# Weighted copies of one edge set on GpSimd: three tensor-scalar operations or one tensor-tensor operation

## The chip, the core and the metric

The kernel runs on one core of a Trainium2 chip. The metric is the device time of one launch in microseconds (us). The core's engines run side by side, each through its own list of instructions, and meet at semaphores: TensorE (PE in the profile, its weight loads PEld) multiplies, VectorE (DVE) and ScalarE (ACT) work on tiles, GpSimd (POOL) does too, and SyncE (SP) issues most transfers.

## The reference, cut to what matters

Four graph layers run over one graph of 3125 nodes (256 features) and 50000 edges sorted by their target. Each layer sums source rows into target rows, plain or weighted by the edge:

```python
# layer 0, twice: agg = segment_sum(h[src], dst); agg / max(deg, 1) @ W_l + b + h @ W_r
# layer 1:
gathered = support[edge_col] * edge_val[:, None]
out = jax.ops.segment_sum(gathered, edge_row, num_segments=x.shape[0])
# layer 2: segment_sum of messages (node and edge features), then an MLP with two layer norms
# layer 3: segment_sum of the 32 largest features of each row, divided by the degree
```

With A[d, s] the number of edges from s to d, and B[d, s] the sum of their weights, every such sum over node rows is a product with A or B. The kernel builds both matrices first and then multiplies with them.

## The kernel before

The edges are cut into 391 tiles of 128. Targets are cut into 25 blocks of 128 nodes, each into 8 groups of 16, so there are 200 groups; each is built by one call of `build_pair` on PE, and the text calls it a pair (it is fed by two kinds of sets). A set of an edge tile is a 128x128 one-hot matrix S (which row an edge belongs to), three copies of S in which each edge's row is multiplied by one of three bf16 parts of its weight, and a one-hot matrix Q of columns. S times Q adds to the counts, each weighted S times Q adds to the weights. All of this lies in `ring`, a part of `e_buf`.

A pair has three parts in the order of PE:

- **first**: the last tile of the pair before, against the first 200 columns (4 matmuls of 200 columns);
- **rest**: the tiles of this pair alone, one in 181 pairs and two in 19, in a loop whose bounds are read from a table on the chip (4 matmuls of 400 columns for each tile);
- **middle**: the tile that this pair shares with the next position, held in `next_set(par, 0..3)` (4 matmuls of 400 columns).

Who makes what for pair n:

- VectorE (`hot_pair`): Q of the first part (L997, 200 columns), S of the middle set (L993, it releases GpSimd through `s_hotS`), then for each rest tile S (L993), S times the first weight part (L1013) and Q (L997, 400 columns), and last Q of the middle set (L997, 400 columns). It waits for `s_used`, so that a buffer is written again only two pairs later.
- GpSimd (`weigh_pair`, L620): the three weighted copies of the middle set. It first copies the tile's three weight columns into `w_col` (L623), drains, waits for S, and then multiplies S by each column (L628, three operations). PE waits for them at L1404. After the seventh pair of a block it also does a subtraction of 256 columns, `second` (L617), for the first layer.
- ScalarE: the other two weighted copies of a rest tile (L669, L670), and the copies of the finished groups out of PSUM (L659, L660).

Buffers alternate by `par`, and the order on every engine is the order of the code: no scheduler moves anything. Once in 8 pairs each engine reads the next 8 table entries. PE also does a transpose (L1412) and a small product (L1418, L1420) once a block. When the 200 pairs are done, PE goes on to the layers, in the same list of instructions.

Of the kernel before, what the change touches and what calls it, by code (L numbers as in the profile page):

```python
# [7 lines left out]
F32, F16, BF16, I32 = mybir.dt.float32, mybir.dt.float16, mybir.dt.bfloat16, mybir.dt.int32  # L8
# [3 lines left out]
P = 128  # L12
# [16 lines left out]
SETS = 4 * P  # L29
# [28 lines left out]
def build(nc, x, src, dst, edge_attr, edge_weight, w, out):  # L58
    ctx = ExitStack()
    with ctx:  # L60
        def sb(name, shape, dt):
            return ctx.enter_context(nc.sbuf_tensor(name, shape, dt))

        def sem(name):
            return ctx.enter_context(nc.semaphore(name))
# [41 lines left out]
        col = front[:, 0:6 * NCOL].rearrange("p (a t) -> p a t", a=6)  # L107
        C_T, C_S, C_Q, C_W0, C_W1, C_W2 = range(6)
# [4 lines left out]
        ring = e_buf[:, 0:RINGW].bitcast(BF16)  # L113
        assert RINGW <= e_partw + e_hotw
        late = {}
        at = NCOL
# [12 lines left out]
        iota1 = sb("iota1", [P, GW], F16)  # L129
        off_g = sb("off_g", [P, NG], F32)  # L130
        off_n = sb("off_n", [P, NT], F32)
        w_col = sb("w_col", [P, 2, 3], F32)
        e_raw = sb("e_raw", [P, EC, DE], F32)
        e_key = sb("e_key", [P, EC], F32)
        e_sum = sb("e_sum", [P, DE], F32)
# [56 lines left out]
        s_hotP = sem("weighted_s_of_pool_ready")  # L192
# [69 lines left out]
        def wait(e, s, v):  # L262
            if not isinstance(v, int):
                e.wait_ge(s, e.snap(v))
            elif v > 0:
                e.wait_ge(s, v)

        def long_loop(e, count):

            return nc.Fori(0, count, engines=[e.engine], hint_back_edge=True)  # L270
# [41 lines left out]
        def drained(e):  # L312

            def step(ins):
                e.drain()
            return step
# [17 lines left out]
        def span(ap, start, width):  # L334
            return ap[:, start:start + width] if isinstance(start, int) else ap[:, bass.ds(start, width)]
# [4 lines left out]
        def bounded(v, low, high):  # L340
            return nc.s_assert_within(v, low, high, skip_runtime_bounds_check_because="the table is clamped to it")
# [20 lines left out]
        def next_set(par, part):  # L362

            at = par * SETS + part * P
            return ring[:, at:at + P]

        def rest_set(i, part):

            at = REST_AT + i % SLOTS * SETS + part * P
            return ring[:, at:at + P]  # L370
# [14 lines left out]
        def pairs_of(e, kind, c, which):  # L385

            lo, many = (0, PER) if which == "rest" else (PER, PER) if which == "fixed" else (0, 2 * PER)
            at = c * (2 * PER) + lo  # L390
            _, packed = nc.values_load_multi_w_load_instructions(
                tab[0:1, at:at + many] if isinstance(c, int) else tab[0:1, bass.ds(at, many)],
                engines=[kind], min_val=0, max_val=ET * 512 + ET + 1,
                skip_runtime_bounds_check_because="the table is clamped to it")
            return packed
# [4 lines left out]
        def low_of(e, v):  # L400
            return bounded(e.snap(v & 511), 0, ET)
# [175 lines left out]
        @block.gpsimd  # L577
        def _(pool):
            chain = drained(pool)
            pool.memset(rows_i[:, 0, EB - 1, :], 0).then_inc(s_pad, 1)  # L580
            pool.memset(rows_i[:, 1, EB - 1, :], PAD_DST).then_inc(s_pad, 1)
            pool.memset(rows[:, 2, EB - 1, :], 0.0).then_inc(s_pad, 1)
            pool.memset(X[:, NT - 1, :], 0.0).then_inc(s_xpad, 1)
            pool.memset(e_raw[:, :, :], 0.0).then_inc(s_pad, 1)
            chain(pool.memset(ident[:, :], 0.0))
            pool.affine_select(out=ident[:, :], in_=ident[:, :], compare_op=ALU.not_equal, fill=1.0, base=0,
                               pattern=[[-1, P]], channel_multiplier=1).then_inc(s_const, 1)
            pool.iota(iota1[:, :], pattern=[[1, GW]], base=1, channel_multiplier=0,
                      allow_small_or_imprecise_dtypes=True).then_inc(s_const, 1)
            pool.iota(off_g[:, :], pattern=[[GW, NG]], base=0, channel_multiplier=0,  # L590
                      allow_small_or_imprecise_dtypes=True).then_inc(s_const, 1)
            pool.iota(off_n[:, :], pattern=[[P, NT]], base=0, channel_multiplier=0,
                      allow_small_or_imprecise_dtypes=True).then_inc(s_const, 1)
            pool.iota(nidx[:, :].rearrange("p (b k) -> p b k", k=2), pattern=[[2 * P, 2], [1, 2]], base=0,
                      channel_multiplier=2,
                      allow_small_or_imprecise_dtypes=True).then_inc(s_const, 1)
            pool.memset(zeros[:, :], 0.0).then_inc(s_const, 1)
            pool.memset(ea_now[:, :], 0.0)
            pool.memset(eps_outer, LN_EPS).then_inc(s_const, 1)
            pool.memset(eps_inner, LN_EPS_INTER).then_inc(s_const, 1)  # L600
            pool.memset(ones_row[:, :], 1.0).then_inc(s_const, 1)
            pool.memset(ring[:, REST_AT + (SLOTS - 1) * SETS:REST_AT + SLOTS * SETS], 0.0)
            pool.memset(col[:, :, 0:1], 0.0).then_inc(s_const, 1)

            pool.memset(ZH[0].rearrange("p (n k) -> p n k", k=ZW)[:, :, 2 * D:2 * D + 2], 1.0).then_inc(s_ones, 1)
            pool.wait_ge(s_rs, 1)
            chain(pool.tensor_scalar(h_all, rs_all, H_SCALE, None, ALU.mult))
            pool.tensor_tensor(shift_all, nmean_all, h_all, ALU.mult).then_inc(s_rs, 1)  # L610
            pool.wait_ge(s_prep, PREP_STEPS)
            pool.wait_ge(s_prep_pe, PE_TABLES + 2)

            def second(n):
                wait(pool, s_z0, n + 1 + CR)
                pool.sem_inc(s_made, 1)
                pool.tensor_tensor(span(ZH[0], n * ZW + D, D), own_row, span(ZH[0], n * ZW, D), ALU.subtract  # L617
                                   ).then_inc(s_z2, 1)

            def weigh_pair(c, i, v):  # L620
                n, par = c * PER + i, i % 2
                w = w_col[:, par, :]
                pool.tensor_copy(w, col[:, C_W0:C_W2 + 1, bass.ds(low_of(pool, v), 1)].rearrange("p a o -> p (a o)"))  # L623
                pool.drain()
                wait(pool, s_hotS, n + 1)
                pool.sem_inc(s_made, 1)
                for k in range(3):
                    m = pool.tensor_scalar(next_set(par, k + 1), next_set(par, 0), w[:, k:k + 1], 1.0,  # L628
                                           ALU.mult, ALU.mult)
                m.then_inc(s_hotP, 1)  # L630

            with long_loop(pool, NT) as c:
                packed = pairs_of(pool, mybir.EngineType.Pool, c, "fixed")
                for i in range(PER):
                    weigh_pair(c, i, packed[i])
                    if i == 6:
                        second(c)


            def mlp_sums(n):  # L640
                for l in range(3):
                    wait(pool, s_y, n * 3 + (l + 1))
                    pool.tensor_tensor(GT[l + 1], GT[l], YT, ALU.add).then_inc(s_g, 1)  # L643

            with pool.Fori(0, NT) as n:
                mlp_sums(n)
# [234 lines left out]
        def _(dve):  # L881
# [118 lines left out]
            def hot_pair(c, i, v, fixed_):  # L1000
                n, par = c * PER + i, i % 2
                k_reg = step_of[mybir.EngineType.DVE]
                wait(dve, s_used, n * 2 + 1)
                edge_cols(n, q_first(par), HW, high_of(dve, fixed_), s_hotQ)
                u = low_of(dve, fixed_)
                wait(dve, s_used, n * 2 + 2)
                edge_rows(next_set(par, 0), u, s_hotS)

                dve.reg_add(room, k_reg, 1)
                with dve.Fori(high_of(dve, v), end_of(dve, v)) as t:  # L1010
                    wait(dve, s_restused, dve.snap(room, min_val=1, max_val=1 << 20))
                    edge_rows(rest_set(i, 0), t, s_restS)
                    dve.tensor_scalar(rest_set(i, 1), iota1[:, 0:P], one(col[:, C_S, :], t), one(col[:, C_W0, :], t),  # L1013
                                      ALU.is_equal, ALU.mult)
                    edge_cols(n, q_rest(par), GW, t, s_restQ)
                    dve.reg_add(k_reg, k_reg, 1)
                    dve.reg_add(room, k_reg, 2)
                edge_cols(n, q_next(par), GW, u, s_hotQ)
# [683 lines left out]
```

## Time and profile before

| what | us |
|---|---|
| median of 3 runs (1706.76 to 1711.73) | 1709.41 |
| the profiled execution, its own time | 1709.9 |
| its span in the trace | 1708.1 |
| building the two matrices, from 47.7 to 480.0 in the trace | 432.3 |
| the same for one of the 25 blocks (8 pairs), mean | 17.3 |

Columns of the rows below: a group of instructions has its line, engine, operation, what it writes and reads, shapes and count, then busy us and mean ns of one, then the idle time of the engine before them and who ended it. A row of a timeline has its start, its length, and what ran, "x3" being three in a row put together; brackets tell of idle time before it and of who ended it. Starts and lengths are us from the start of the span. An operation's length begins when the engine takes it up, so it holds any time in which it stands and waits for its data; the next one is taken up some 0.08 us before the end of the one ahead.

### The profile page before, as it was taken

To read this page: it belongs to the slowest core of one execution; us is meant where nothing else is said; L and a number is where in the kernel's file an instruction comes from. 1 tells how busy PE (TensorE), PEld (TensorE's weight loads), DVE (VectorE), ACT (ScalarE), POOL (GpSimd) and SP (SyncE) were. 2 spreads that over 40 slices of the span, in tenths; PEclk is the share of its full clock that TensorE was granted. 3 is DMA by queue.
4 is the path that set the end of the run, shared out by engine and by line. 5 is a ranking of instruction groups with operands and counts; after the bars stand their busy time and mean duration, and the time that the engine had idled before them with its cause. 6 is when DMAs were issued, how large, how long until landed. Compare 5 with 4: busy or idle time off the path is not lost.

```text
span 1708.1 us, 41810 instructions
## 1 busy us (share of the span) xinstructions
PE 1587.9 (93%) x11011; PEld 1227.7 (72%) x11012; DVE 960.3 (56%) x2841; ACT 625.3 (37%) x1718; POOL 326.2 (19%) x926
## 2 busy tenths in 40 slices
PE   2899999999988999899999999999899999977996
PEld 1555565555666777588878888888778888855885
DVE  5788888888842222233336666666537777773111
ACT  6677787777721111111112222222234444430000
POOL 1565565655610000000000000000011111110000
PEclk8899999999999999999999999999999999988998
DMA  4266676757696666333355655566322212211444
GB/s 133 70 179 170 156 193 164 186 155 195 163 255 202 193 193 194 127 120 130 122 161 155 178 160 159 163 179 174 108 82 80 76 64 80 80 39 62 150 153 152
DMA packets 353541, 245.55 MB, mean 144 GB/s; under 512 B 195243, under 2 KB 337383, under 8 KB 353511
## 3 DMA queue, kind: packets, MB, share of 16 engines
q1 hardware_dynamic: 353510, 245.19, 50.1%
q8 instruction: 14, 0.23, 0.1%
q14 instruction: 17, 0.13, 0.0%
HBM read 138.17 MB, written 99.31 MB: 139 GB/s over the span
## 4 chain that ended last, share of the span: by engine, by line
issue 60%; PE 33%; DVE 3%; POOL 2%; DVEq 1%; SPq 0%; POOLq 0%; DMA 0%; ACT 0%
PE ps L1377 21%; PE ps L1466 8%; POOL work L643 2%; PE ps L1420 1%; PE ps L1418 1%; DVE e_buf L997 0%; DVE work L943 0%; PE ps L1412 0%; PE ps L1639 0%; SPq L419 0%; PE ps L1353 0%; DVE small L1253 0%; PE ps L1365 0%; DVE e_buf L1013 0%; PE ps L1370 0%
## 5 line engine op out<-in xcount | busy, mean ns | idle before, releaser
L1466 PE MATMUL ps<-arena 128*128 128x256 f16 (+1 forms) x5000 | 605.3, 274 | 18.3 <-DVE arena L1317 8.9
L1466 PEld LDWEIGHTS ps<-arena 128*128 128x128 f16 x5000 | 488.1, 98 | 115.5 <-issue 47.2
L1377 PE MATMUL ps<-e_buf 128*128 128x400 bf16 (+1 forms) x2476 | 374.8, 308 | 23.6 <-DVE e_buf L997 23.5
L1377 PEld LDWEIGHTS ps<-e_buf 128*128 128x128 bf16 x2476 | 217.6, 98 | 169.6 <-DVE e_buf L997 51.6
L1460 PE MATMUL ps<-arena 128*128 128x256 f32 x1250 | 279.6, 381 | 0.6 <-ACT arena L791 0.6
L1460 PEld LDWEIGHTS ps<-arena 128*128 128x128 f32 x1250 | 236.5, 191 | 32.3 <-ACT arena L791 0.9
L628 POOL TENSOR_SCALAR e_buf<-e_buf,w_col 128x128 bf16<-128x128 bf16 x600 | 220.9, 382 | 162.5 <-DVE e_buf L993 156.1
L643 POOL TENSOR_TENSOR work<-work 128x256 f32<-128x256 f32 x75 | 54.4, 726 | 1000.7 <-ACT work L836 1000.7
L997 DVE TENSOR_SCALAR e_buf<-iota,off_g,front 128x400 bf16<-128x400 f16 (+1 forms) x619 | 222.3, 405 | 35.0 <-PE ps L1377 30.6
L993 DVE TENSOR_SCALAR e_buf<-iota,front 128x128 bf16<-128x128 f16 x419 | 111.4, 273 | 40.5 <-PE ps L1377 26.8
L669 ACT ACTIVATE e_buf<-e_buf,front 128x128 bf16<-128x128 bf16 x219 | 88.3, 403 | 106.8 <-DVE e_buf L993 106.4
L1142 DVE TENSOR_SCALAR rdeg<-ps 128x1 f32 (+1 forms) x25 | 4.0, 159 | 172.1 <-PE ps L1466 162.3
L660 ACT ACTIVATE arena<-ps 128x400 f32<-128x400 f32 x200 | 99.5, 498 | 0.0
L659 ACT ACTIVATE work<-ps 128x400 f16<-128x400 f32 x200 | 98.1, 490 | 1.3 <-PE ps L1377 1.3
L747 ACT ACTIVATE work<-ps 128x256 f32<-128x256 f32 x75 | 28.8, 383 | 175.7 <-PE ps L1440 175.7
L670 ACT ACTIVATE e_buf<-e_buf,front 128x128 bf16<-128x128 bf16 x219 | 85.3, 390 | 0.0
L1617 PE MATMUL ps<-work,front 128*128 128x128 f32 x600 | 81.6, 280 | 3.3 <-POOL work L643 3.2
L742 ACT ACTIVATE small<-small 128x1 f32<-128x1 f32 x50 | 14.7, 294 | 186.1 <-DVE small L1030 186.1
L1617 PEld LDWEIGHTS ps<-work,front 128*128 128x128 f32 x600 | 74.9, 196 | 7.0 <-POOL work L643 4.7
L1333 DVE SCALAR_TENSOR_TENSOR work<-ps,rdeg,arena 128x256 f32<-128x256 f32 x25 | 12.1, 484 | 113.2 <-PE ps L1466 113.2
L1013 DVE TENSOR_SCALAR e_buf<-iota,front 128x128 bf16<-128x128 f16 x219 | 75.1, 343 | 0.0
L836 ACT ACTIVATE work<-ps,mlp_col 128x128 f32<-128x128 f32 x150 | 46.8, 364 | 58.0 <-PE ps L1617 58.0
(214 smaller groups left out, 1580.4 us busy)
## 6 DMA issues: line engine op xcount, KB each, us to landing
arena<-turned_blocks SPq DMA_DIRECT2D x75, 800.0 KB, 4.3
wgt_blocks<-arena SPq DMA_DIRECT2D x25, 1600.0 KB, 10.3
arena<-wgt_blocks SPq DMA_DIRECT2D x25, 1600.0 KB, 8.3
cnt_blocks<-work SPq DMA_DIRECT2D x25, 800.0 KB, 5.6
turned_blocks<-arena SPq DMA_DIRECT2D x25, 800.0 KB, 3.5
e_raw<-edge_features_padded SPq DMA_DIRECT2D x25, 576.0 KB, 7.8
edge_features_padded<-in_edge_attr SPq DMA_DIRECT2D x24, 512.0 KB, 9.9
out<-arena SPq DMA_DIRECT2D x24, 128.0 KB
```

The lines of the kernel that those rows point to most:

```text
L628: m = pool.tensor_scalar(next_set(par, k + 1), next_set(par, 0), w[:, k:k + 1], 1.0, ALU.mult, ALU.mult)
L643: pool.tensor_tensor(GT[l + 1], GT[l], YT, ALU.add).then_inc(s_g, 1)
L659: act.activation(stage_c[par][:, t, :], cnt_ps[t % 2][:, 0:GW], ACT.Copy)
L660: act.activation(stage_w[par][:, t, :], wgt_ps[t % 2][:, 0:GW], ACT.Copy).then_inc(s_taken, 1)
L669: act.activation(rest_set(i, 2), rest_set(i, 0), ACT.Copy, scale=one(col[:, C_W1, :], t))
L670: act.activation(rest_set(i, 3), rest_set(i, 0), ACT.Copy, scale=one(col[:, C_W2, :], t)).then_inc(s_restA, 1)
L993: return dve.tensor_scalar(into, iota1[:, 0:P], one(col[:, C_S, :], t), None, ALU.is_equal).then_inc(s_S, 1)
L997: dve.tensor_scalar(into, iota1[:, 0:wide], one(off_g, n), one(col[:, C_Q, :], t), ALU.add, ALU.is_equal).then_inc(s_Q, 1)
L1377: return pe.matmul(bank[:, 0:wide], rows_, cols, start=start, stop=True, skip_group_check=True)
L1460: m = pe.matmul(agg[par][:, 0:D], BLK32[par][:, b * P:(b + 1) * P], ZFULL[0][:, b * D:(b + 1) * D], start=(b == 0), stop=(b == NT - 1), sk ...
L1466: m = pe.matmul(agg[par][:, 0:wide], BLK16[par][:, b * P:(b + 1) * P], ZH[zin(i)][:, b * ZW + part * D:b * ZW + part * D + wide], start=(b ...
L1617: m = pe.matmul(mlp_ps[:, o * P:(o + 1) * P], W[:, k, o * P:(o + 1) * P], GT[l][:, k * P:(k + 1) * P], start=(k == 0), stop=(k == 1))
```

## The change

GpSimd's three operations for a pair become one. Its first operand is S read three times over (a step of zero between the three), its second the three weight columns straight from `col`, each repeated over 128 columns, and it writes 3 x 128 columns in one go. `w_col`, the copy into it and the drain are gone. Nothing on another engine is touched.

```diff
-        w_col = sb("w_col", [P, 2, 3], F32)
...
+        def next_sets(par, part, many):
+
+            at = par * SETS + part * P
+            return ring[:, at:at + many * P]
+
...
             def weigh_pair(c, i, v):
                 n, par = c * PER + i, i % 2
-                w = w_col[:, par, :]
-                pool.tensor_copy(w, col[:, C_W0:C_W2 + 1, bass.ds(low_of(pool, v), 1)].rearrange("p a o -> p (a o)"))
-                pool.drain()
+                factors = col[:, C_W0:C_W2 + 1, bass.ds(low_of(pool, v), 1)].broadcast_to([P, 3, P])
+                plain = next_set(par, 0).rearrange("p (o n) -> p o n", o=1).broadcast_to([P, 3, P])
                 wait(pool, s_hotS, n + 1)
                 pool.sem_inc(s_made, 1)
-                for k in range(3):
-                    m = pool.tensor_scalar(next_set(par, k + 1), next_set(par, 0), w[:, k:k + 1], 1.0,
-                                           ALU.mult, ALU.mult)
-                m.then_inc(s_hotP, 1)
+                pool.tensor_tensor(next_sets(par, 1, 3).rearrange("p (a n) -> p a n", n=P), plain, factors, ALU.mult
+                                   ).then_inc(s_hotP, 1)
```

GpSimd's list of instructions, before, around the subtraction after a block's seventh pair (`s_ready` is the semaphore of the finished S; REGISTER_ALU and ISA are work of its sequencer, here the address of the tile's weight columns):

```order
L628 TENSOR_SCALAR e_buf<-e_buf,w_col 128x128 [waits s_ready]
L628 TENSOR_SCALAR e_buf<-e_buf,w_col 128x128 x2
L264 REGISTER_ALU
L617 ISA [waits first_part_ready]
L617 REGISTER_ALU
L617 TENSOR_TENSOR arena<-arena 128x256
L623 REGISTER_ALU
L623 ISA
L623 COPY w_col<-front 128x3
```

The same place after the change:

```order
L263 REGISTER_ALU
L630 REGISTER_ALU [waits s_ready]
L630 ISA
L630 TENSOR_TENSOR e_buf<-e_buf,front 128x384
L263 REGISTER_ALU
L621 ISA [waits first_part_ready]
L621 REGISTER_ALU
L621 TENSOR_TENSOR arena<-arena 128x256
```

The work on the address moved from ahead of the wait for S to behind it, and one operation of 384 columns stands where three of 128 stood.

## Rows read from the trace of the kernel before

**Rows 1.** The page, its head and busy times of the engines.
```profile
span 1708.1 us, 41810 instructions
PE 1587.9 (93%) x11011; PEld 1227.7 (72%) x11012; DVE 960.3 (56%) x2841; ACT 625.3 (37%) x1718; POOL 326.2 (19%) x926
```

**Rows 2.** Windows: start:end, length, engines' busy us, PE clock, DMA; the build.
```profile
47.00:480.00 433.00, 412.71 (x2671) 247.24 (x2671) 359.00 (x1259) 333.76 (x935) 266.91 (x825) 0.99 0.65 167
```

**Rows 3.** The chain that ended last, between 200 and 275 us: start, us, what.
```profile
204.96 0.62 PE ps L1418 x2
...
222.66 0.62 PE ps L1418 x2
...
238.33 0.62 PE ps L1418 x2
238.95 1.06 PE ps L1420 x4
240.01 8.53 PE ps L1377 x60
248.54 0.22 PE ps L1412 x2
248.76 5.16 PE ps L1377 x36
253.92 0.62 PE ps L1418 x2
```

**Rows 4.** Who waited for whom from 60 to 440 us: us, times, longest.
```profile
PE ps L1377 <- DVE e_buf L997: 17.0, 17, 1.1
```

**Rows 5.** Who waited for GpSimd's L628 in the whole span: us, times.
```profile
  PEld ps L1377: 0.2, 1
```

**Rows 6.** Timeline of VectorE, then of GpSimd, through one pair.
```profile
212.57 0.31 DVE L997 TENSOR_SCALAR e_buf<-iota,off_g,front 128x200 bf16<-128x200 f16 x1
212.81 0.24 DVE L993 TENSOR_SCALAR e_buf<-iota,front 128x128 bf16<-128x128 f16 x1
...
213.18 0.31 DVE L1013 TENSOR_SCALAR e_buf<-iota,front 128x128 bf16<-128x128 f16 x1
213.41 0.38 DVE L997 TENSOR_SCALAR e_buf<-iota,off_g,front 128x400 bf16<-128x400 f16 x1
213.72 0.42 DVE L997 TENSOR_SCALAR e_buf<-iota,off_g,front 128x400 bf16<-128x400 f16 x1
214.06 0.38 DVE L997 TENSOR_SCALAR e_buf<-iota,off_g,front 128x200 bf16<-128x200 f16 x1
214.35 0.24 DVE L993 TENSOR_SCALAR e_buf<-iota,front 128x128 bf16<-128x128 f16 x1
...
213.25 1.12 POOL L628 TENSOR_SCALAR e_buf<-e_buf,w_col 128x128 bf16<-128x128 bf16 x3 [0.56 <-DVE e_buf L993]
```

**Rows 7.** GpSimd's groups by shape, whole span.
```profile
L628 POOL TENSOR_SCALAR e_buf<-e_buf,w_col 128x128 bf16<-128x128 bf16 x600 | 220.9, 382 | 162.5 <-DVE e_buf L993 156.1 <-issue 6.3
L643 POOL TENSOR_TENSOR work<-work 128x256 f32<-128x256 f32 x75 | 54.4, 726 | 1000.7 <-ACT work L836 1000.7
...
L617 POOL TENSOR_TENSOR arena<-arena 128x256 f32 x25 | 16.3, 651 | 0.0
...
L610 POOL TENSOR_TENSOR arena<-arena 128x25 f32<-128x25 f32 x1 | 0.2, 229 | 0.1
```

**Rows 8.** GpSimd's sequencer at L623: count, ns least/median/most, first and last start.
```profile
L623 POOLq ALU_OP  x200: 32/35/45, 47.1 to 476.1; - x100
L623 POOLq FUSED_REGOPS  x200: 46/46/52, 47.2 to 476.2; - x100
```

**Rows 9.** Timelines of GpSimd and VectorE around two of the 25 subtractions L617.
```profile
64.26 0.66 POOL L617 TENSOR_TENSOR arena<-arena 128x256 f32 x1
...
64.27 0.70 DVE L993 TENSOR_SCALAR e_buf<-iota,front 128x128 bf16<-128x128 f16 x1
...
305.89 0.67 POOL L617 TENSOR_TENSOR arena<-arena 128x256 f32 x1
...
305.96 0.67 DVE L997 TENSOR_SCALAR e_buf<-iota,off_g,front 128x200 bf16<-128x200 f16 x1
306.56 0.41 DVE L993 TENSOR_SCALAR e_buf<-iota,front 128x128 bf16<-128x128 f16 x2
```

**Rows 10.** Timeline of VectorE at a block's first pair.
```profile
309.23 0.33 DVE L997 TENSOR_SCALAR e_buf<-iota,off_g,front 128x200 bf16<-128x200 f16 x1 [1.34 <-PE ps L1377]
```

## The prediction

> **What bounds the kernel now.** I read the page first, then the build alone, then its chain, its waits, and one pair as a timeline. The page shows a span of 1708.1 us with PE busy for 93% [rows 1]; the change touches only the build of the two matrices, the 433 us in which GpSimd makes the weighted copies. There PE is busy for 412.71 us and VectorE for 359.00 [rows 2], so two engines are close to the bound and GpSimd is not. The chain says how close: in a block without a split pair (a pair with two rest tiles) it is PE and nothing else. The block from 238.33 to 253.92 is 0.62 + 1.06 + 8.53 + 0.22 + 5.16 = 15.59 us, with no hole [rows 3]. Sixty matmuls of L1377 are five pairs, so a pair costs PE 8.53 / 5 = 1.71 us; the other 1.90 us of the block are the small products. The block from 204.96 to 222.66 has one split pair and takes 17.70. Where PE does wait, it waits for VectorE's L997: 17.0 us in 17 waits [rows 4]. For GpSimd's three products PE's weight loads waited once, for 0.2 us [rows 5]. Making GpSimd faster therefore buys nothing by itself; what counts is what GpSimd does to VectorE, which has to deliver a pair every 1.71 us.
>
> VectorE's slack is small. In the pair shown, the middle S starts at 212.81 and that of the next pair at 214.35: 1.54 us, against PE's 1.71 [rows 6].
>
> **What goes, and what stands in its place.** The copy and the drain leave GpSimd's list, 200 times each. They lie off the path [rows 5], so they are worth nothing. The three L628 took 1.12 us together [rows 6]. The new operation isn't in the trace; the nearest rows are GpSimd's other two-operand operations: 229 ns for 25 columns (L610), 651 for 256 (L617), 726 for 256 with both operands f32 (L643) [rows 7]. Through L610 and L617 a column costs (651 - 229) / 231 = 1.83 ns, so 384 columns take 651 + 128 x 1.83 = 885 ns. With L643 it is (726 - 229) / 231 = 2.15 ns, and 726 + 275 = 1001. I take 0.89, since L617 mixes f32 with a 16-bit operand as the new operation does. The low end is 0.65: no shorter than L617, although it has more columns. Repeated reads (steps of zero) are in no row; I price them as ordinary ones.
>
> The Trainium skill (GPSIMD Engine Reference, section 3.1) has 4497 ns for a two-operand addition of 2048 columns, 2.2 ns per column, as the floor of its shared read port. As an estimate that makes 384 columns 0.84 us; L643's rate here, 2.15, agrees. By 0.84 the sum below would be +28 in place of +37.
>
> A second effect comes from the order: the address of the weight columns is now worked out behind the wait for S. These are two steps of GpSimd's sequencer, 35 and 46 ns [rows 8], so the operation starts 0.08 later than L628 did. L628 started 213.25 - 212.81 = 0.44 after S did; the new one starts at 0.52 and ends at 0.52 + 0.89 = 1.41. Before, the third product ended at 0.44 + 1.12 = 1.56. PE gets its weighted sets a little earlier, so no new wait at L1404, and no gain there either.
>
> **What the long operation holds up.** This is the term that decides. L617 is the one two-operand operation that GpSimd runs in the build, and the rows beside it show what VectorE does meanwhile. L617 ran from 305.89 to 306.56. VectorE's L997 of 200 columns began at 305.96 and lasted 0.67, where the same shape takes 0.33 when left alone [rows 9, 10]: it ended 0.07 after L617 did. The other case is the same: L993 began 0.01 after L617 and lasted 0.70 in place of 0.24 [rows 6, 9]. VectorE didn't slow down, it stood until GpSimd was done. With three short operations VectorE slips one of its own between two of GpSimd's: L1013 took 0.31 and the two L997 0.38 and 0.42 beside the three L628 [rows 6]. With one long operation there is no such gap.
>
> The Trainium skill (SBUF — State Buffer, section "Who interferes with whom") has the rule: a VectorE instruction in a two-port mode and a GpSimd instruction lock each other out for the whole instruction, without sharing. The 0.67 agrees. By it the sum is the one below; if the two merely shared the port, VectorE would stay under 1.71 us and the sum would be zero.
>
> Now which instruction is caught. An L997 of 200 columns needs the port 0.26 after its start (0.33 less the 0.07 by which the held one outlasted L617). Applied to the pair shown, the new operation runs from 213.33 to 214.22. L1013 began at 213.18 and needs the port at about 213.44; the L997 of the rest tile began at 213.41 and needs it at 213.67. The L993 of 64.27 would have needed it within its 0.24 and was held, so GpSimd takes the port at most 0.2 after its start, here by 213.53. So L1013 gets through and L997 is caught, until 214.22. It ends 0.12 later (0.07, and 0.05 for 200 more columns: 0.38 against 0.33), and the next is taken up 0.08 before that, 0.04 after GpSimd's end. From there the order is as now: L997 of the middle set to L997 of the next pair 214.06 - 213.72 = 0.34, less the 0.04 by which that L997 was stretched (0.42 for 0.38), so 0.30; then to the next S 212.81 - 212.57 = 0.24 [rows 6].
>
> **The sum.** From S to S VectorE needs 0.44 + 0.08 + 0.89 + 0.04 + 0.30 + 0.24 = 1.99 us, over PE's 1.71: VectorE sets the pace. Two things are added in a block. L617 still holds one instruction for 0.67 in place of 0.33, +0.34; now PE's work covers it, then nothing does. And at a block's first pair VectorE idles for 1.34 while its sequencer reads the table [rows 10]; the row names PE, but the table is read there. While the engine is held for 214.22 - 213.67 = 0.55 its sequencer works ahead, so I count 1.34 - 0.55 = 0.8. A block takes 8 x 1.99 + 0.34 + 0.8 = 17.06 us in place of 15.59, +1.47. PE's 1.90 us of small products are hidden then. I take the same +1.47 for the blocks with split pairs, whose extra wait between the two tiles stays. 25 x 1.47 = 37 us. All later stages stand behind the build in PE's list, so they move as a whole. The profiled execution's own time was 1709.9, 0.5 above the median of the runs: 1709.9 + 37 = 1747, and 1709.4 + 37 = **1746** for the median.
>
> At 1.00 us the cycle is 2.10, the block 8 x 2.10 + 0.34 + 0.7 = 17.8, and the sum +56: 1765. At 0.65 it is 1.75; the block 14.0 + 0.34 + 1.0 = 15.3 is under PE's 15.59, and nothing changes: 1709. The break-even lies near 0.69 us for the operation.
>
> **The rivals.** *More is caught.* If GpSimd takes the port before L1013 does (a start 0.1 earlier is enough), L1013 is held and the rest L997 comes after it: 0.31 (213.41 to 213.72) less what is already counted, about 0.24 more per pair, 8 x 0.24 x 25 = 48 us: 1794. The same happens if the repeated operands make the operation some 0.25 us longer. Against it: L1013 got through although L628 had begun 0.07 after it.
>
> *Nothing is caught that counts.* If the operation is under 0.69 us, or takes the port more than 0.34 after its start, so that the rest L997 passes too, only the last L997 is held, the cycle is 1.99 - 0.31 = 1.68, and PE stays the bound: 1709. Against it: both rows of L617.
>
> *Faster.* Now GpSimd takes the port three times per pair and a copy's worth besides; one short take would leave VectorE freer than now. What there is to gain is PE's waiting for L997, 17.0 us in 380 [rows 4], 19 in the whole build; most of it belongs to the split pairs, whose second tile waits for the first. Half of it would give 1700. It decides from an operation near 0.6 us, which would be shorter than L617 with half as many columns again.
>
> That the change doesn't take place is no rival: the order shows one operation of 384 columns per pair.
>
> **How the numbers follow.** Forecast (one instruction held per pair, 1715 to 1770): 0.62. More held: 0.12. Nothing changes: 0.16. Faster: 0.10. The measurement can tell about 0.3%, 5 us, from no change. So slower 0.74, same 0.16, faster 0.10. The range reaches from 1709, the low end of the operation's price, to 1785, which takes in its high end and a third of the way to the case with more held; about 0.1 is left out on each side.
>
> **What would show it.** Right: L997 of 400 columns has a mean well over the 0.38 to 0.42 seen now, near 0.7 (every second one held to about 1.0); PE's waits for L997 grow from 17 us to some 50; a plain block takes about 17 us in the chain; GpSimd's new operation is near 0.89; all stages after the build keep their lengths. Wrong: the operation under 0.7, or a mean of L997 near today's; L1013 held instead of L997 (the dearer rival); or a granted clock in the build clearly under today's 0.99 [rows 2], which would add to PE's own time and isn't in the sum.

## The result and the profile after

The changed kernel takes 1754.58 us (median of 4 runs, 1750.62 to 1756.53) where the kernel before took 1708.09 on the same chip: a ratio of 1.0268, with an interval of 1.024 to 1.0296. It is slower by 46 us; the prediction had 1746, between 1709 and 1785. The profiled run took 1755.56, its span grew from 1708.1 to 1753.7, by 45.6.

In the new file the lines are shifted: L993, L997, L1013, L1377, L1412, L1418 and L1420 are now one higher, the subtraction L617 is L621, the reading of the table on VectorE is L395, and the new operation is L630. First the head of the page and its line of busy times, then the build alone as one stretch (columns as in rows 2: PE, PEld, DVE, ACT, POOL, granted clock, DMA share, GB/s).

```profile
span 1753.7 us, 41010 instructions
...
PE 1604.8 (92%) x11011; PEld 1226.3 (70%) x11012; DVE 1038.7 (59%) x2841; ACT 635.0 (36%) x1718; POOL 252.5 (14%) x326
```

```profile
48.00:534.00 486.00, 433.27 (x2672) 248.57 (x2672) 437.64 (x1259) 343.86 (x937) 193.26 (x225) 0.99 0.58 152
```

Against [rows 1, 2]: the build is 53 us longer (485.4 in place of 432.3, from 48.1 to 533.5), and the granted clock in it is 0.99 in both, so the clock has no part. GpSimd's busy time in the build fell by 74 us, from 266.91 to 193.26. VectorE's rose by 79, from 359.00 to 437.64, with the same 1259 instructions. GpSimd does its work faster, and VectorE pays for it. Which instructions pay is seen in the groups by shape. GpSimd over the whole span, after:

```profile
L630 POOL TENSOR_TENSOR e_buf<-e_buf,front 128x384 bf16<-128x384 bf16 x200 | 175.2, 876 | 291.9 <-DVE e_buf L994 291.9
...
L621 POOL TENSOR_TENSOR arena<-arena 128x256 f32 x25 | 19.0, 761 | 0.0
```

VectorE from 60 to 480 us, first after, then the two groups of before that answer to it:

```profile
L998 DVE TENSOR_SCALAR e_buf<-iota,off_g,front 128x400 bf16<-128x400 f16 x364 | 212.9, 622 | 0.0
L1014 DVE TENSOR_SCALAR e_buf<-iota,front 128x128 bf16<-128x128 f16 x190 | 83.3, 438 | 0.0
L994 DVE TENSOR_SCALAR e_buf<-iota,front 128x128 bf16<-128x128 f16 x364 | 79.3, 246 | 33.7 <-PE ps L1378 29.3 <-issue 4.0
L998 DVE TENSOR_SCALAR e_buf<-iota,off_g,front 128x200 bf16<-128x200 f16 x174 | 56.2, 323 | 8.8 <-PE ps L1378 4.8 <-issue 2.4
```

```profile
L997 DVE TENSOR_SCALAR e_buf<-iota,off_g,front 128x400 bf16<-128x400 f16 x410 | 164.7, 437 | 0.0
L1013 DVE TENSOR_SCALAR e_buf<-iota,front 128x128 bf16<-128x128 f16 x213 | 73.2, 343 | 0.0
```

The 400-column operation went from a mean of 437 ns to 622, L1014 from 343 to 438; S and the 200-column operation, made while GpSimd is idle, stand at 246 and 323. The timeline shows the two ways in which this comes about, in two pairs that follow each other (VectorE, then GpSimd; start, length, what ran, x2 and x3 being so many instructions in one row):

```profile
264.81 0.30 DVE L1014 TENSOR_SCALAR e_buf<-iota,front 128x128 bf16<-128x128 f16 x1
265.04 1.05 DVE L998 TENSOR_SCALAR e_buf<-iota,off_g,front 128x400 bf16<-128x400 f16 x1
...
267.36 0.88 DVE L1014 TENSOR_SCALAR e_buf<-iota,front 128x128 bf16<-128x128 f16 x1
268.16 0.37 DVE L998 TENSOR_SCALAR e_buf<-iota,off_g,front 128x400 bf16<-128x400 f16 x1
```

```profile
265.06 0.91 POOL L630 TENSOR_TENSOR e_buf<-e_buf,front 128x384 bf16<-128x384 bf16 x1 [1.36 <-DVE e_buf L994]
267.36 0.83 POOL L630 TENSOR_TENSOR e_buf<-e_buf,front 128x384 bf16<-128x384 bf16 x1 [1.39 <-DVE e_buf L994]
```

In the first pair L1014 passes in 0.30 and the 400-column L998 of the rest tile starts at 265.04, 0.02 before GpSimd's operation, and stands until that is done: it ends at 266.09, 0.12 after GpSimd's 265.97. That is the forecast's case. In the second L1014 itself starts with GpSimd, lasts 0.88, and the whole rest tile comes after it: the dearer rival. Of the 181 pairs with one rest tile, L998 of the rest tile was held in 128 and L1014 in 48 (both in 2 of them). GpSimd seems to wait too: 77 of its 200 operations took 0.83 us, the other 123, nearly all begun beside an L1014 that was still at work, 0.88 and more; the mean of 0.876 holds this time.

The chain of waits in a plain block, to be held against [rows 3] (start, length, what the end hung on):

```profile
245.57 0.62 PE ps L1419 x2
246.19 1.06 PE ps L1421 x4
247.25 3.74 PE ps L1378 x28
250.99 1.54 PE ps L1378 x8
...
253.99 1.03 DVE e_buf L998
255.07 1.53 PE ps L1378 x8
...
260.55 1.04 DVEq L395
...
263.16 0.62 PE ps L1419 x2
```

From 245.57 to 263.16 it is 17.59 us, where it was 15.59. It is no longer PE alone: the chain crosses to VectorE, and the two long pieces there are a held L998 of 1.03 us and, before the next block, 1.04 us in which VectorE's sequencer (DVEq) reads the table while another L998 is held, from 260.56 to 261.58. GpSimd isn't on it: the profile puts the held time down to VectorE. PE's own waits, 60 to 480 us, first before, then after, and below them who waited for L630 over the whole span:

```profile
PE ps L1377 <- DVE e_buf L997: 18.0, 18, 1.1
```

```profile
PE ps L1378 <- DVE e_buf L998: 45.7, 122, 1.1
```

```profile
  PEld ps L1378: 0.2, 1
```

PE waits for VectorE 122 times and 45.7 us, where it was 18 times and 18.0 us. For the weighted sets it waited once, 0.2 us, as before [rows 5].

**Part of it is given back after the build.** The build ends 53.5 us later in the trace, the program 45.6. The first work of VectorE after the build is the reciprocal degree; it waits for the last block of counts to come back from memory. Before, then after:

```profile
494.20 0.16 DVE L1142 TENSOR_SCALAR rdeg<-ps 128x1 f32<-128x1 f32 x1 [9.75 <-DMA cnt_blocks<-work]
```

```profile
544.47 0.16 DVE L1143 TENSOR_SCALAR rdeg<-ps 128x1 f32<-128x1 f32 x1 [6.57 <-DMA cnt_blocks<-work]
```

It comes 14.2 us after the end of the build before, and 11.0 after it now. The last store of counts is issued by SP, before and after, behind transposed loads:

```profile
467.32 12.95 SPq L472 DMA_TRANSPOSE arena<-cnt_blocks  x2
...
486.56 0.43 SPq L463 DMA_DIRECT2D cnt_blocks<-work  x1
```

```profile
517.53 12.82 SPq L476 DMA_TRANSPOSE arena<-cnt_blocks  x2
...
536.28 0.43 SPq L467 DMA_DIRECT2D cnt_blocks<-work  x1
```

That was 6.6 us after the end of the build and is 2.8 now: the store stands on SP's queue behind two transposed loads of the blocks before (12.95 us before, 12.82 after). They ended 0.3 us after the end of the build before, and 3.2 ahead of it now: a longer block hides more of them. When the opening of the first layer is over the shift is down to 47.7; the later stages differ by some 2 us in either direction, which I can't put to one cause.

### The profile page after: what moved, and what is told of

Same layout as the page of the kernel before. It is cut to its first block, busy times and chain, and to the rows that moved or that the text cites. A ratio compares the mean times of both kernels' runs of the same rounds, so it can differ in the third digit from the quotient of the medians.

```text
span 1753.7 us, 41010 instructions
## 1 busy us (share of the span) xinstructions
PE 1604.8 (92%) x11011; PEld 1226.3 (70%) x11012; DVE 1038.7 (59%) x2841; ACT 635.0 (36%) x1718; POOL 252.5 (14%) x326
## 4 chain that ended last, share of the span: by engine, by line
issue 60%; PE 25%; DVE 8%; DVEq 3%; POOL 2%; SPq 0%; POOLq 0%; DMA 0%; ACT 0%
PE ps L1378 14%; PE ps L1467 8%; DVE e_buf L998 4%; POOL work L644 2%; PE ps L1421 1%; DVE e_buf L994 1%; PE ps L1419 1%; DVEq L395 1%; DVEq L998 1%; DVEq L994 1%; DVE e_buf L1014 1%; DVEq L1011 0%; DVEq L1010 0%; DVE work L944 0%; PE ps L1413 0%
## 5 line engine op out<-in xcount | busy, mean ns | idle before, releaser
L1378 PE MATMUL ps<-e_buf 128*128 128x400 bf16 (+1 forms) x2476 | 394.9, 308 | 56.6 <-DVE e_buf L998 56.1
L998 DVE TENSOR_SCALAR e_buf<-iota,off_g,front 128x400 bf16<-128x400 f16 (+1 forms) x619 | 296.1, 525 | 10.8 <-PE ps L1378 4.8
L630 POOL TENSOR_TENSOR e_buf<-e_buf,front 128x384 bf16<-128x384 bf16 x200 | 175.2, 876 | 291.9 <-DVE e_buf L994 291.9
L1014 DVE TENSOR_SCALAR e_buf<-iota,front 128x128 bf16<-128x128 f16 x219 | 96.7, 442 | 0.0
```

The lines of the kernel that those rows point to most:

```text
L630: pool.tensor_tensor(next_sets(par, 1, 3).rearrange("p (a n) -> p a n", n=P), plain, factors, ALU.mult).then_inc(s_hotP, 1)
L998: dve.tensor_scalar(into, iota1[:, 0:wide], one(off_g, n), one(col[:, C_Q, :], t), ALU.add, ALU.is_equal).then_inc(s_Q, 1)
L1378: return pe.matmul(bank[:, 0:wide], rows_, cols, start=start, stop=True, skip_group_check=True)
```

## The experiments

The theory: one GpSimd instruction, from its start to its end, keeps VectorE's operations waiting that read SBUF as these do, and 0.88 us of that in one piece is more than VectorE's slack. The rivals: it is the two-operand kind, or the repeated reads, or the later start, whatever the length; or GpSimd's result is late for PE.

**Three short operations of the same kind.** The new operation is cut into three of 128 columns; the kind, the operands, the address worked out late and the missing copy stay. Only the repeated read of S goes with the cut; the next two kernels have it.

```diff
-                plain = next_set(par, 0).rearrange("p (o n) -> p o n", o=1).broadcast_to([P, 3, P])
...
-                pool.tensor_tensor(next_sets(par, 1, 3).rearrange("p (a n) -> p a n", n=P), plain, factors, ALU.mult
-                                   ).then_inc(s_hotP, 1)
+                for k in range(3):
+                    m = pool.tensor_tensor(next_set(par, k + 1), next_set(par, 0), factors[:, k, :], ALU.mult)
+                m.then_inc(s_hotP, 1)
```

> The one operation of 384 columns is cut into three of 128, each still two-operand and straight from the weight columns; nothing else differs from the changed kernel. Theory (one long hold of VectorE): three holds of about 0.25 us with gaps between them, one VectorE instruction passes in each gap; the L998 of 400 columns fall from a mean of 0.62 us to under 0.50; total within 10 us of the kernel before, 1708 to 1718. Rival (what costs is that GpSimd reads two operands, or that the address is worked out behind the wait, however long one operation is): both are unchanged, so the total stays near 1755.

Measured: 1711.21, against 1708.59 for the kernel before beside it, a ratio of 1.0015 (1.0002 to 1.0027). GpSimd's and VectorE's groups from 60 to 480 us, and PE's wait in the same stretch:

```profile
L630 POOL TENSOR_TENSOR e_buf<-e_buf,front 128x128 bf16<-128x128 bf16 x579 | 221.9, 410 | 183.0 <-DVE e_buf L994 183.0
```

```profile
L998 DVE TENSOR_SCALAR e_buf<-iota,off_g,front 128x400 bf16<-128x400 f16 x404 | 176.4, 473 | 0.0
```

```profile
PE ps L1378 <- DVE e_buf L998: 19.7, 27, 1.1
```

An operation of 128 columns takes 0.41 us, and not the 0.25 that was expected. So a pair keeps GpSimd busy for 3 x 0.41 = 1.23 us in place of 0.88, and still the loss is all but gone: L998 is back at 473 ns, PE waits 19.7 us. Busy time, kind of operation and late address are out as causes of the 46 us; the length of a single instruction is left, and the repeated read, which the next two kernels keep.

**How the loss grows with the length.** Two kernels with an instruction of middle length. In the first the two-operand operation makes two copies instead of three, and PE uses the second twice; in the second, which is the kernel before, one one-operand operation makes all three copies from the first weight part.

```diff
-                factors = col[:, C_W0:C_W2 + 1, bass.ds(low_of(pool, v), 1)].broadcast_to([P, 3, P])
...
+                factors = col[:, C_W0:C_W1 + 1, bass.ds(low_of(pool, v), 1)].broadcast_to([P, 2, P])
...
-                pool.tensor_tensor(next_sets(par, 1, 3).rearrange("p (a n) -> p a n", n=P), plain, factors, ALU.mult
+                pool.tensor_tensor(next_sets(par, 1, 2).rearrange("p (a n) -> p a n", n=P), plain, factors, ALU.mult
...
-                product(weights, GW, next_set(par, 3), q_next(par)).then_inc(s_used, 1)
+                product(weights, GW, next_set(par, 2), q_next(par)).then_inc(s_used, 1)
```

> GpSimd makes two of the three weighted copies in one operation of 256 columns; the third is left out, and PE multiplies the second copy twice, so all its work stays. Theory: the operation takes about 0.65 us, just under the break-even of 0.69 that the prediction gave, so most of the 46 us are gone: 1708 to 1719. Rival (any single two-operand operation in place of the three short ones costs the same): near 1755. If the cost is simply proportional to columns: 1739.

```diff
-                for k in range(3):
-                    m = pool.tensor_scalar(next_set(par, k + 1), next_set(par, 0), w[:, k:k + 1], 1.0,
-                                           ALU.mult, ALU.mult)
-                m.then_inc(s_hotP, 1)
+                plain = next_set(par, 0).rearrange("p (o n) -> p o n", o=1).broadcast_to([P, 3, P])
+                pool.tensor_scalar(ring[:, par * SETS + P:par * SETS + 4 * P].rearrange("p (a n) -> p a n", n=P), plain,
+                                   w[:, 0:1], 1.0, ALU.mult, ALU.mult).then_inc(s_hotP, 1)
```

> The kernel before with its three one-operand multiplications put into one of 384 columns with repeated reads; all three copies get the first weight part, so the weights differ. Copy and drain stay. Theory: what counts is how long one operation holds VectorE. Between 25 and 128 columns a column of a one-operand operation cost 0.8 to 0.9 ns, so it takes 0.57 to 0.62 us and the total stays at the kernel before, 1706 to 1713. Rival (any one long operation costs as much as the changed kernel's): 1750 and more. If it takes over 0.8 us the theory wants 1725 or more.

Measured: 1714.32, 1.0037 (1.0023 to 1.0051), for the first; 1714.72, 1.0034 (1.002 to 1.0048), for the second, a little over the range that was expected of it. GpSimd's group, 60 to 480 us, in the first and in the second:

```profile
L630 POOL TENSOR_TENSOR e_buf<-e_buf,front 128x256 bf16<-128x256 bf16 x191 | 122.0, 639 | 283.2 <-DVE e_buf L994 283.2
```

```profile
L628 POOL TENSOR_SCALAR e_buf<-e_buf,w_col 128x384 bf16<-128x384 bf16 x194 | 119.6, 617 | 247.5 <-DVE e_buf L992 247.5
```

An instruction of 0.62 to 0.64 us costs some 6 us, one of 0.88 costs 46: two thirds of the columns, an eighth of the price. That is a threshold and not a rate, as it must be where VectorE has slack to lose first. Beyond it nearly all counts: 0.876 - 0.639 = 0.24 us more in 200 pairs is 47 us, and 40 came. At this length it also doesn't matter whether the operation has one operand or two, nor whether it follows a copy; and both kernels read S repeatedly, so that alone isn't the cause either. The forecast's break-even of 0.69 was a little high, since 6 us are lost already at 0.62.

**The copy kept.** The new operation, with its factors from the copied weight columns; the copy and the drain are back, and no address stands between S and the operation.

```diff
+        w_col = sb("w_col", [P, 2, 3], F32)
...
-                factors = col[:, C_W0:C_W2 + 1, bass.ds(low_of(pool, v), 1)].broadcast_to([P, 3, P])
+                w = w_col[:, par, :]
+                pool.tensor_copy(w, col[:, C_W0:C_W2 + 1, bass.ds(low_of(pool, v), 1)].rearrange("p a o -> p (a o)"))
+                pool.drain()
+                factors = w.rearrange("p (a o) -> p a o", o=1).broadcast_to([P, 3, P])
```

> The one operation of 384 columns, but its factors come from the copied columns again, with the copy and the drain, so that no address is worked out behind the wait for S. This undoes the order part of the change alone. Theory: the operation starts 0.10 to 0.12 us earlier after S, the hold stays as long (0.87), and VectorE's cycle shortens by that much where it is held at the rest tile's L998: 8 x 0.1 x 25 = 20 to 24 us back, 1731 to 1736. Rival (the earlier start lets GpSimd take the port ahead of L1014 in most pairs, the dearer catch of the prediction): 1755 to 1790. Rival (copy and drain cost something of their own): slower than the changed kernel.

Measured: 1762.59, 1.0313 (1.0296 to 1.033). The theory's gain from an earlier start didn't come; the first rival did, and the second isn't ruled out. GpSimd's and VectorE's groups from 60 to 480 us (four lines were added ahead, so S is L998 here, L1018 the rest tile's S times the first weight part, and L1002 the 400-column operation), and one pair:

```profile
L634 POOL TENSOR_TENSOR e_buf<-e_buf,w_col 128x384 bf16<-128x384 bf16 x171 | 141.7, 829 | 223.8 <-DVE e_buf L998 223.8
```

```profile
L1018 DVE TENSOR_SCALAR e_buf<-iota,front 128x128 bf16<-128x128 f16 x189 | 142.8, 756 | 0.0
...
L1002 DVE TENSOR_SCALAR e_buf<-iota,off_g,front 128x400 bf16<-128x400 f16 x359 | 129.8, 398 | 0.0
```

```profile
302.55 0.98 DVE L1018 TENSOR_SCALAR e_buf<-iota,front 128x128 bf16<-128x128 f16 x1
```

```profile
302.65 0.83 POOL L634 TENSOR_TENSOR e_buf<-e_buf,w_col 128x384 bf16<-128x384 bf16 x1 [1.32 <-DVE e_buf L998]
```

The operation starts 0.43 us after S in place of 0.58, and catches an earlier instruction: L1018 is held in 134 of the 181 pairs with one rest tile (mean 756 ns) and in 49 the rest tile's S, still one earlier; together that is every one of the 181. The 400-column operation is free again (398). All that follows on VectorE then stands behind the hold. The operation itself was even shorter, 0.83. Yet the fourth to the sixth pair of a block take VectorE 2.06 to 2.07 us, against 2.03 to 2.05 in the changed kernel: what the dearer catch costs, the earlier start gives back. In these pairs the start was worth nothing either way; where the 8 us over the changed kernel come from, the copy on GpSimd included, wasn't taken apart.

**Taking VectorE's reads off SBUF.** If it is a hold between the two engines on their way to SBUF, then a VectorE operation that reads its index row from PSUM might not be held. The index row is copied to an idle PSUM bank once, and VectorE's three one-hot operations read it there, in the kernel before and in the changed one.

```diff
+            iota_ps = ps[:, 6, 0:GW]
+            dve.tensor_copy(iota_ps, iota1[:, :])
+            dve.drain()
...
-                return dve.tensor_scalar(into, iota1[:, 0:P], one(col[:, C_S, :], t), None, ALU.is_equal
+                return dve.tensor_scalar(into, iota_ps[:, 0:P], one(col[:, C_S, :], t), None, ALU.is_equal
...
-                dve.tensor_scalar(into, iota1[:, 0:wide], one(off_g, n), one(col[:, C_Q, :], t),
+                dve.tensor_scalar(into, iota_ps[:, 0:wide], one(off_g, n), one(col[:, C_Q, :], t),
...
-                    dve.tensor_scalar(rest_set(i, 1), iota1[:, 0:P], one(col[:, C_S, :], t), one(col[:, C_W0, :], t),
+                    dve.tensor_scalar(rest_set(i, 1), iota_ps[:, 0:P], one(col[:, C_S, :], t), one(col[:, C_W0, :], t),
```

Of the kernel before:

> VectorE's one-hot operations read the row of indices from PSUM instead of SBUF (copied there once), with GpSimd as before. This is the base for the next run. VectorE's operations become longer for themselves, L997 of 400 columns some 0.5 us, so VectorE sets the pace and the total rises: 1725 to 1760. Theory: without its SBUF read VectorE no longer needs what GpSimd takes, so its operations have one length each, whether GpSimd runs or not.

Of the changed one:

> The same with GpSimd's one operation of 384 columns, as in the changed kernel. Theory (VectorE is held because both need the same port into SBUF): with VectorE's reads out of SBUF there is no hold, and this kernel equals the run before it within 6 us, though the two original kernels are 46 us apart; L998 and L1014 have one length each. Rival (VectorE's writes into SBUF, or something else in GpSimd's long operation, hold it): again some 40 to 50 us over the run before it.

Measured: 1810.37, 1.06 (1.0581 to 1.0619), and 1808.31, 1.0592 (1.0573 to 1.0611). The first time is far over its range, since I had put the PSUM-fed operation at about 0.5 us and it takes 0.68; that the two kernels would come out equal holds. VectorE's 400-column group from 60 to 480 us, before with PSUM, then after with PSUM, and GpSimd's operations in the latter:

```profile
L1000 DVE TENSOR_SCALAR e_buf<-ps,off_g,front 128x400 bf16<-128x400 f32 x327 | 210.5, 681 | 0.0
```

```profile
L1001 DVE TENSOR_SCALAR e_buf<-ps,off_g,front 128x400 bf16<-128x400 f32 x327 | 210.5, 682 | 0.0
...
L1017 DVE TENSOR_SCALAR e_buf<-ps,front 128x128 bf16<-128x128 f32 x170 | 67.7, 398 | 0.0
```

```profile
L630 POOL TENSOR_TENSOR e_buf<-e_buf,front 128x384 bf16<-128x384 bf16 x156 | 129.8, 832 | 277.0 <-DVE e_buf L997 277.0
L621 POOL TENSOR_TENSOR arena<-arena 128x256 f32 x20 | 13.1, 655 | 0.0
```

VectorE sets the pace in both by its own length. Its 400-column operations take 681 and 682 ns, whether GpSimd runs three short instructions beside them or one of 0.83, and its three other groups are as alike (339, 474 and 398 ns in both): no hold is left. Nor does GpSimd wait: all 200 of its operations take 832 to 834 ns, and the subtraction is back at 655. VectorE still writes its results to SBUF here and reads its one-column operands there, so that alone isn't what is locked.

The Trainium skill (SBUF — State Buffer, section "Who interferes with whom") says that a VectorE instruction with at most one SBUF input, outside its two-port modes, doesn't contend with GpSimd. The equal 681 and 682 agree; that it is the mode, and not the place it reads from, no run here shows.

**Only the caught instruction.** The rest tile's 400-column operation alone reads PSUM, in the changed kernel and, for the price of the edit, in the kernel before. The row is copied to PSUM as in the two kernels above.

```diff
...
-            def edge_cols(n, into, wide, t, s_Q):
-                dve.tensor_scalar(into, iota1[:, 0:wide], one(off_g, n), one(col[:, C_Q, :], t),
+            def edge_cols(n, into, wide, t, s_Q, iota=iota1):
+                dve.tensor_scalar(into, iota[:, 0:wide], one(off_g, n), one(col[:, C_Q, :], t),
...
-                    edge_cols(n, q_rest(par), GW, t, s_restQ)
+                    edge_cols(n, q_rest(par), GW, t, s_restQ, iota_ps)
```

> The changed kernel, but VectorE's one instruction that was caught most, the rest tile's L998 of 400 columns, reads its indices from PSUM; all others read SBUF as before. Theory: that instruction now takes 0.68 us for itself and runs while GpSimd has the port, so the cycle is 0.55 (S to this L998) + 0.60 + 0.30 + 0.24 = 1.69 us, about PE's 1.71; most of the 46 us go although GpSimd's operation stays at 0.83 to 0.88: 1709 to 1725, the rest being pairs whose L1014 is caught. Rival (the hold is of VectorE as a whole while GpSimd's long operation runs): 1755 or more.

> The same edit on the kernel before, with its three short operations. Theory: here nothing is held for long, so the slower read from PSUM is a loss, or nothing where PE's work covers it: 1708 to 1725. It is the base for the run before it: theory wants the two within 12 us of each other, the rival 46 us apart.

Measured: 1712.32, 1.0028 (1.0014 to 1.0042), of the changed kernel; 1708.38, 1.0009 (0.9995 to 1.0022), of the one before. The changed kernel's rows, 60 to 480 us, VectorE and GpSimd:

```profile
L1001 DVE TENSOR_SCALAR e_buf<-ps,off_g,front 128x400 bf16<-128x400 f32 x207 | 142.0, 686 | 0.0
...
L1017 DVE TENSOR_SCALAR e_buf<-iota,front 128x128 bf16<-128x128 f16 x207 | 77.0, 372 | 0.0
L1001 DVE TENSOR_SCALAR e_buf<-iota,off_g,front 128x400 bf16<-128x400 f16 x190 | 70.9, 373 | 0.0
```

```profile
L630 POOL TENSOR_TENSOR e_buf<-e_buf,front 128x384 bf16<-128x384 bf16 x190 | 158.2, 833 | 248.5 <-DVE e_buf L997 248.5
```

This is the change as it was, its one operation of 384 columns included (0.83 us), with one VectorE instruction per rest tile made slower (686 ns in place of 373) and out of the hold's way. 42 of the 46 us are gone. By the time it ends GpSimd is done, so the next one, of the middle set, runs in 373. What is left, 4 us against the same edit on the kernel before, may belong to L1017, which is still held in 22 pairs, each the first of its block; that wasn't taken apart.

No version beat the kernel before: its plain blocks stand at PE's own 15.59 [rows 3], and what PE waits for there belongs to pairs with two rest tiles. Removing the copy and the drain alone, with three one-operand operations on the weight columns where they lie, wasn't tried and stays open.

## Why the prediction was right, point by point

- **What bounds the kernel.** Right: GpSimd's own speed bought nothing (0.2 us of waiting for it in both), and its 74 us less in the build show nowhere in the time. VectorE was the engine with too little slack.
- **The operation.** 0.89 was forecast from L610 and L617, 0.876 measured; but the operation alone takes 0.83, the rest is its own waiting for VectorE, so part of the closeness is luck. Repeated reads of S cost nothing extra: 128 columns, with S read once, took 410 ns, 256 and 384 with S repeated 639 and 876, nearly on one line; L617, without any repeats, took 651 for 256 [rows 7].
- **The mechanism.** Right, and shown from three sides: cutting the instruction removes nearly all of the loss, shortening it removes most, and taking the caught instruction's reads off SBUF does too.
- **What is caught.** Partly: L998 of the rest tile in 128 of 181 pairs, but the dearer L1014 in 48, where the forecast had none. It falls mostly on the first pair of a block (22 of 22 with one rest tile) and the third (15 of 23). In all 48 VectorE had fallen behind: the rest tile's S began 0.41 us or more after the middle one and L1014 0.58 or more, together with GpSimd's operation; in the other 133 it was 0.16 and 0.32. Why VectorE pauses just there wasn't tested. "A start 0.1 earlier is enough" was right as a mechanism: the kernel with the copy kept showed it, in every pair with one rest tile. Its price of 1794 was too high, 1762.59 came: the 0.24 us per pair left out that the earlier start also ends the hold earlier.
- **The sum.** The terms were mis-sized in both directions. From S to S a pair with one rest tile took, by its place in the block, a mean of 2.21, 2.23, 2.15, 2.05, 2.03, 2.05, 2.48 and 2.37 us, together 17.57 where the forecast had 17.06:

| term | forecast us | measured us | difference per block |
|---|---|---|---|
| cycle with L998 caught | 1.99 | 2.03 | 8 x 0.04 = +0.32 |
| dearer catch, pairs 1 to 3 | 0 | 2.21 + 2.23 + 2.15 - 3 x 2.03 | +0.50 |
| pairs 4 to 6 | 0 | 2.05 + 2.03 + 2.05 - 3 x 2.03 | +0.04 |
| the subtraction's hold | 0.34 | 2.48 - 2.03 = 0.45 | +0.11 |
| the table read | 0.80 | 2.37 - 2.03 = 0.34 | -0.46 |

The cycle is longer since the operation starts 0.58 after S and not 0.52: moving the address behind the wait cost some 0.13 and not the 0.08 of its two steps. The subtraction costs more since it now follows a longer operation, and the middle set's L998 stood behind it in 22 of the 24 pairs at that place. The table is read while VectorE stands, more than I had allowed: in the block of the chain 1.04 of the reading lie beside a held L998, and VectorE then idles 0.11 us before the next block's first instruction, where the forecast kept 0.8.
- **Split blocks.** Wrong: they were given a plain block's +1.47. A block with one split pair went from a median of 17.77 to 20.23, +2.46. PE's wait between the two tiles is for VectorE, which is itself held there; I read that from the waits and didn't test it. Measured from S to S, the 13 plain blocks went from 15.63 to a mean of 17.45, 24 us together, and the 12 with split pairs bring the rest of the build's 53. Of the 16 us by which the build's loss was forecast too small, some 12 are theirs and some 4 the plain blocks'.
- **"All later stages move as a whole."** Wrong by 8 us, and that is why a build that lost 53 where 37 was forecast gave a time only 9 us over it. The forecast looked at PE's list alone. The store of the last block, for which the next layer waits, stands behind SP's loads, which a longer block covers better: 3 of the 8 us come there, 2 to 3 more in the opening of the first layer; what brings the rest is open. With that, part of the closeness of 1746 to 1754.58 is two errors of opposite sign.
- **The signs named ahead.** A mean of L998 near 0.7: 0.62. PE's waits some 50: 45.7. A plain block about 17: 17.6. The operation near 0.89: 0.876. The clock: unchanged. One sign named as wrong came in part: L1014 held in 48 of 181 pairs. And the stages after the build didn't all keep their lengths.

## What to carry to other kernels

Judge an operation on GpSimd by how long each single one keeps VectorE off, not by what they add up to: three of 0.41 us cost some 3 us here and one of 0.88 cost 46. Before joining small operations into a long one, look in the timeline for the VectorE instructions beside GpSimd's longest one, and hold the length of the new one against VectorE's slack per round. And ask of a longer stage what it hides for the next one; not every microsecond that it loses reaches the end.

## What the runs showed of the hardware that was not expected

- A 400-column comparison on VectorE that reads its row as f32 from PSUM takes 0.68 us, against 0.37 to 0.38 as f16 from SBUF when nothing holds it, and isn't held beside a GpSimd operation of 0.83. For the one instruction that is caught it is the cheaper choice; for all of them it costs 100 us.
- The hold works both ways: the subtraction on GpSimd, L621, grew from 651 to 761 ns in the changed kernel. It now follows the long operation at once, and a VectorE instruction that had been standing goes first, by the timeline. With VectorE's index reads in PSUM it takes 655 again, and L630 832 to 834 ns in all 200 pairs, where it had been 830 to 1048.
- One GpSimd operation with one tensor operand over 384 columns takes 617 ns; with two it is 876. The single operations over 128 columns differ less, 382 ns [rows 7] against 410.
